# Where two groups of matmul operands begin in SBUF: projection weights and the ring of transposed inputs, in a graph-attention layer

## The reference, cut to what matters

```python
def layer(h, adjacency, W_left, b_left, W_self, b_self, W_right, b_right, gamma, beta):
    u = einsum('bld,bmd->blm', h, h) / sqrt(d)
    p = softmax(u, axis=-1)
    delta = p * adjacency
    attn = delta / (sum(delta, axis=2, keepdims=True) + 1e-10)
    h_left  = einsum('bld,ed->ble', h, W_left)  + b_left
    h_self  = einsum('bld,ed->ble', h, W_self)  + b_self
    h_right = einsum('bld,ed->ble', h, W_right) + b_right
    # above the diagonal: left; on it: self; below it: right
    ctx = attn_left @ h_left + diag(attn)[..., None] * h_self + attn_right @ h_right
    o = (ctx - mean(ctx)) / sqrt(var(ctx) + 1e-12) * gamma + beta
    return relu(o)
x = layernorm(x + layer(x, adj, ...))
```

## Time and profile before

| | us |
|---|---|
| median of 3 runs | 462.38 |
| lowest, highest | 462.02, 462.85 |
| the profiled execution | 462.62 |
| its span | 460.9 |
| TensorE busy in the span | 450.7 (98%) |
| VectorE, ScalarE, GpSimd busy | 383.0, 321.5, 209.4 |
| mean granted clock of TensorE | 0.995 |

### The profile page before, as it was taken

How to read it: one execution, slowest core, us unless ns; L and a number is a source line. 1 busy time by engine, 2 the same in 40 slices (tenths; PEclk the granted TensorE clock), 3 DMA queues, 4 the chain that set the end, 5 groups by cost and what they waited for, 6 DMA issues and landing times.

```text
span 460.9 us, 9449 instructions
## 1 busy us (share of the span) xinstructions
PE 450.7 (98%) x2639; PEld 448.4 (97%) x2639; DVE 383.0 (83%) x1117; ACT 321.5 (70%) x710; POOL 209.4 (45%) x293
## 2 busy tenths in 40 slices
PE   8999999999999999999999999999999999999992
PEld 8999999999999999999999999999999999999992
DVE  5877888888888878988878988878889887987876
ACT  6756677677677677678677677677677777767752
POOL 0144445543345553345554345554344653344542
PEclk9999999999999999999999999999999999999998
DMA  8765356566455665555666555566445566454322
GB/s 255 225 206 181 118 178 195 189 196 192 144 180 184 189 193 173 174 171 182 188 193 198 152 172 183 183 206 193 154 159 194 176 216 193 144 175 141 102 70 79
DMA packets 84134, 80.59 MB, mean 175 GB/s; under 512 B 7058, under 2 KB 76436, under 8 KB 84116
## 3 DMA queue, kind: packets, MB, share of 16 engines
q1 hardware_dynamic: 84112, 80.38, 54.7%
q10 hardware_dynamic: 4, 0.00, 0.0%
HBM read 52.04 MB, written 28.31 MB: 174 GB/s over the span
## 4 chain that ended last, share of the span: by engine, by line
issue 28%; POOL 21%; DVE 14%; PE 14%; ACT 11%; DMA 6%; SPq 5%; POOLq 0%; DVEq 0%; ACTq 0%
PE ps_proj L484 8%; POOL scaled L1112 7%; POOL shifted L1116 6%; DMA dt_raw<-dt_dram 5%; POOL rstd L1106 5%; ACT normed L639 4%; SPq L321 3%; DVE y_sb L867 3%; ACT ps_scores L590 3%; DVE proj_lo L819 3%; PE ps_ctx L528 3%; POOL dt_right L1100 2%; DVE delta L799 2%; DVE cross_turned L767 2%; POOL dt_left L1100 2%
## 5 line engine op out<-in xcount | busy, mean ns | idle before, releaser
L484 PE MATMUL ps_proj<-w_hi,xt_split 128*128 128x384 f32 x1152 | 304.8, 336 | 0.1
L484 PEld LDWEIGHTS ps_proj<-w_hi,xt_split 128*128 128x128 f32 x1152 | 209.1, 188 | 0.7 <-ACT ps_proj L609 0.5
L484 PE MATMUL ps_proj<-w_lo,xt_split 128*128 128x384 f32 x576 | 193.6, 336 | 0.0
L1106 POOL TENSOR_TENSOR rstd<-var_eps,minus_half 128x4 f32<-128x4 f32 x31 | 36.5, 1177 | 187.8 <-DVE var_eps L853 187.8
L484 PEld LDWEIGHTS ps_proj<-w_lo,xt_split 128*128 128x128 f32 x576 | 108.3, 188 | 0.0
L609 ACT ACTIVATE ps_proj<-bias 128x386 f32<-128x386 f32 (+1 forms) x188 | 90.5, 495 | 1.5 <-DVE proj_lo L819 1.2
L1112 POOL TENSOR_TENSOR scaled<-normed,gamma_sb 128x384 f32<-128x384 f32 x60 | 61.0, 1017 | 30.2 <-ACT normed L639 30.2
L613 ACT ACTIVATE proj_hi<-ps_proj 128x384 fp32r<-128x384 f32 x128 | 63.5, 497 | 11.3 <-PE ps_proj L484 11.0
L633 ACT ACTIVATE ps_ctx<-ps_proj,diag 128x386 f32<-128x386 f32 x64 | 35.7, 557 | 49.1 <-PE ps_proj L484 49.1
L819 DVE TENSOR_TENSOR proj_lo<-ps_proj,proj_hi 128x384 fp32r<-128x384 f32 x128 | 67.4, 544 | 2.1 <-ACT proj_hi L613 2.1
L1116 POOL TENSOR_TENSOR shifted<-scaled,beta_sb 128x384 f32<-128x384 f32 x61 | 61.9, 1015 | 2.5
(11 more groups left out here) (104 smaller groups left out, 640.2 us busy)
## 6 DMA issues: line engine op xcount, KB each, us to landing
x_sb<-in_x SPq DMA_DIRECT2D x32, 384.0 KB, 4.3
xt_sb<-in_x_t SPq DMA_DIRECT2D x31, 384.0 KB, 3.9
out_dram<-out_sb SPq DMA_DIRECT2D x31, 384.0 KB, 2.8
adj_sb<-in_adj SPq DMA_DIRECT2D x32, 256.0 KB, 4.4
dt_dram<-turned SPq DMA_DIRECT2D x31, 256.0 KB, 2.0
dt_raw<-dt_dram SPq DMA_DIRECT2D x124, 64.0 KB, 2.0
cross_dram<-cross_turned SPq DMA_DIRECT2D x29, 256.0 KB, 2.0
cross_raw<-cross_dram SPq DMA_DIRECT2D x116, 64.0 KB, 2.0
```

Of the source, the lines that this page charges most:

```text
L484: mm = nc.tensor.matmul(ps_proj[bank(at, g)][:, 0:H], stationary, moving[w][:, c, :], start=(clear and i == 0), stop=True, skip_group_chec ...
L1106: nc.gpsimd.tensor_tensor(rstd[at.slot(2)][:], var_eps[:], minus_half[:], ALU.pow).then_inc(rstd_ready, 1)
```

## The change

Three tiles are allocated that nothing reads or writes: 64 bytes ahead of the weights, 32 bytes ahead of `xt_split`, 32 bytes ahead of `dt_full`.

```diff
@@ -120,6 +120,8 @@
         ident = sb("ident", [P, P])
         zeros = sb("zeros", [P, HE], F32R)
         minus_half = sb("minus_half", [P, 2 * T])
+
+        sb("weights_place", [P, 16])
         w_raw = [sb(f"w_raw{w}", [P, C, H]) for w in range(3)]
         w_hi = [sb(f"w_hi{w}", [P, C, H], F32R) for w in range(3)]
         w_lo = [sb(f"w_lo{w}", [P, C, H], F32R) for w in range(3)]
@@ -131,6 +133,7 @@
         x_sb = [sb(f"x_sb{i}", [P, T, H]) for i in range(UNROLL)]
         xt_sb = [sb(f"xt_sb{i}", [P, C, L]) for i in range(UNROLL)]
         adj_sb = [sb(f"adj_sb{i}", [P, T, L]) for i in range(UNROLL)]
+        sb("xt_place", [P, 8])
 
         xt_split = [sb(f"xt_split{i}", [P, C, 2 * L], F32R) for i in range(UNROLL)]
         z_sum = [sb(f"z_sum{i}", [P, T]) for i in range(2)]
@@ -151,6 +154,7 @@
         cross_turned = sb("cross_turned", [P, Q * T * T * R])
         cross_raw = sb("cross_raw", [P, Q, T, T * R])
 
+        sb("dt_place", [P, 8])
         dt_full = sb("dt_full", [P, 2, T * T, P], F32R)
         dt_left = sb("dt_left", [P, 2, T, P], F32R)
         dt_right = sb("dt_right", [P, 2, T, P], F32R)
```

## The result

| | before | after |
|---|---|---|
| median, us | 462.38 | 467.29 |
| lowest to highest | 461.94 to 463.03 (5 runs) | 467.12 to 467.5 (5 runs) |
| span of the profiled execution | 460.9 | 465.4 |
| mean granted clock | 0.995 | 0.994 |

The ratio is 1.0099, with a 95% interval from 1.008 to 1.0119: the change makes the kernel slower by 1%, and the time lies in the predicted range of 456.5 to 468.5.

What follows compares the result with a forecast made beforehand. The prediction took TensorE's unbroken matmul stream to bound the kernel. Its terms for projections, scores, attention, other engines and DMA, each 0, summed to no change from the 462.38 us median: 462.4 us, range 456.5 to 468.5.

Steps and rivals of the forecast that it cites:

- What bounds the kernel: Whole kernel: TensorE, busy 98% of the span with 2.3 us of waits, sets the time by its matmuls' start-to-start distance.
- rival C: Projections: both operands beginning at 0 modulo 128 may meet, 173.3 to 176.7 ns each, +5.8 us, 468.2 us; chance 0.23.
- the prediction's own sign: Projections: the prediction is wrong if their distance changes by more than 0.53 ns.
- transfers and other engines: DMA, VectorE and ScalarE at new addresses: cost 0, hidden behind TensorE's unbroken stream.
- The likeliest case: Whole kernel: no change, within 0.2%, 461.5 to 463.3 us; chance 0.45.
- the term of the projections: 1728 projection matmuls with both operands moved to 0 modulo 128: taken as 0, bounds -23.0 and +5.8 us.
- The attention: Attention matmuls, whose operands keep their remainders: taken as 0, bounds 0.9 us either way.
- The scores: Scores matmuls in pieces, both operands moved from 32 to 0: taken as 0, bounds -3.5 and +0.9 us.
- The argument against C: Left and right projections of batch 0: 176.7 and 173.3 ns at the same remainders, so address alone does not set it.
- Rival A: Projections: aligned rows touch 12 blocks of 128 bytes instead of 13, saving 23.0 us, 439.4 us; chance 0.17.
- Rival B: TensorE's stream: other addresses give a shorter rhythm, 3.3 ns less, -5.8 us, 456.6 us (small form 461.2); chance 0.15.
- The formula of the Trainium skill: Projections: a page's gap for a warm stream, 162.5 ns against 173.3 measured; -18.7 us if unaligned operands explain it all.

Runs made afterwards that it cites:

- e5: Against the kernel before, only `xt_split` moved, to the same start modulo 512 as the weights (distance 0): 462.78 us, ratio 1.0006.
- f2: Against the kernel before, `xt_split` moved to begin 256 bytes above the weights modulo 512: 463.18 us, ratio 1.0017.
- f1: The change without the tile ahead of `xt_split`; weights at a multiple of 128, distance 96 as in the kernel before: 467.56 us, ratio 1.0109.
- e1: Against the kernel before, weights alone moved to 0 modulo 128, `xt_split` left at 32: 463.27 us, ratio 1.0013.
- e2: Against the kernel before, `xt_split` alone moved to 0 modulo 128, weights left at 64: 462.25 us, ratio 0.9991.
- e4: Against the kernel before, `xt_split` moved from 32 to 64 modulo 128, where the weights begin (distance 128 modulo 256): 467.25 us, ratio 1.0095.
- f3: Against the kernel before, `xt_split` moved to begin 384 bytes above the weights modulo 512: 466.83 us, ratio 1.0092.
- e8: Against the kernel before, `w_lo` and `xt_split` moved so only the low weight halves have distance 128, the high ones 192: 462.76 us, ratio 1.0006.
- e3: Against the kernel before, weights and `xt_split` both moved up by 32 bytes, their distance kept at 96: 463.34 us, ratio 1.0015.

## Why the prediction was right or wrong

**What bounds the kernel** was right. TensorE's stream sets the time, waits are no larger after, the clock is the same, and the whole difference is in the distance between matmuls. The time of 467.29 us lies in the range only because rival C was taken in; the forecast itself, 462.4 us, is missed by 4.9 us, and by the prediction's own sign (more than 0.53 ns a projection) it is wrong, with 2.8 ns measured. That transfers and other engines cost 0 at their new addresses was right too: `x_sb` lands after 4.4 us (before 4.3), `xt_sb` after 3.8 (before 3.9).

```profile
x_sb<-in_x SPq DMA_DIRECT2D x32, 384.0 KB, 4.4
xt_sb<-in_x_t SPq DMA_DIRECT2D x31, 384.0 KB, 3.8
```

**The likeliest case was wrong**, and the step that failed is the term of the projections: "I take 0, because the rows nearest to an aligned operand show no gain." Those rows, the `zeros` matmul and the scores in pieces, could only speak against a gain. They said nothing against a loss. A single matmul among others cannot show a rhythm, and the scores have both operands in one tile. Both operands of the `zeros` row begin at the same address, which is distance 0, and not the 128 modulo 256 that the change makes: remainders modulo 128 hid the difference. The measured term is 32 x 0.131 = 4.2 us. The 2.8 ns of a long stretch, taken for all 1728, would make 4.8 us, which is more than the whole span grew: the sixth group and the first matmuls behind the attention lose less. The attention, also put at 0, grew by about 0.5 us, within its bound of 0.9. The scores stayed at 0.

**Rival C had the place and nearly the size**: projections, +5.8 us for 3.33 ns each, measured +4.2 us of the +4.9 in all. Its mechanism did not hold, so the near size is luck. It said that both operands begin at 0 and meet; e5 and f2 begin alike modulo 256 and have the short rhythm. It also took the rhythm from batch 0, where each three take 0.53 us. That rhythm belongs to the distance 96, where f1 has it. The change has another, of 880 ns for five.

**The argument against C misread.** "Batch 0 has both rhythms at the same remainders, so the address alone does not set it" is true for a distance of 96, and f1 shows it once more. But I took it as evidence that addresses matter little. It was evidence that this stream has more than one rhythm and can change over, and neighbouring distances (112, 128) no longer have the short one in their long stretches. That the two rhythms at 96 come from standing beside that region is a reading, not shown. A smaller slip in the same place: the `zeros` row shows 0.18 us, which is 6 ns above the usual surplus and not 3 (the starts in ns give 177, which is 3).

**Rival A is refuted.** With weights at a multiple of 128 and a distance of 32 (e1), a row of 1536 bytes still takes 173.3 ns. That 13 blocks of 32 columns give exactly this was a coincidence, or has another cause. **Rival B** found no case: no distance tried went under 6.24 us for 36, so 173.3 ns looks like the floor of this stream. The formula of the Trainium skill, TensorE: Matmul & The Clock Gate, Back-to-back issue gap, N / 2.4 + 2.5 ns, is given there as the gap of an isolated matmul, not of a stream of weight loads and matmuls as here. The 162.5 ns that it would make of 384 columns, an estimate, was reached by none of these placements; none went under 173.3.

**What is shown, and what stays open.** Shown: the projections' spacing is the loss but for some 0.5 us, and only addresses changed. Neither operand's own start brings the loss alone (e1, e2, e4). The distance modulo 256 sorts all kernels but f1, and 128 is slow at three pairs of starts modulo 512, which are two modulo 256 (the change; e4 and f3). Distances 0, 32 and 192 were seen at one pair modulo 256 each. At 96 two kernels are fast and one is slow. Not shown is what it is in the chip. That the read of the moving columns and the load of the next weights disturb each other is an inference from the fact that a distance between those two operands counts. Nor is it known why the region lies around 112 and 128, how far it reaches above 128, and what picks the rhythm at 96.

## What to carry to other kernels

In a dense stream of fp32r matmuls, compare the starts in SBUF of the moving and the stationary operand with each other, modulo 256, and not each with a round number: here distances of 0, 32 and 192 bytes kept the short rhythm in long stretches, and 128 cost 1% of the kernel. An unrelated tile of a few bytes can shift that distance, so a difference of about 1% after such an edit, with no new wait and the same clock, is to be looked for in the start-to-start distance of the matmuls. If the same code runs at two spacings, as here in batch 0, the stream has more than one rhythm, and a few bytes can lose what it has: f1 has the distance of the kernel before and is slow.

## What the runs showed of the hardware that was not expected

- The delays of the stream repeat with a period of their own, which has nothing to do with the program's three: five matmuls (880 ns) at a distance of 128, two (353 ns, in the starts in ns) in f1.
- The start modulo 128 is not enough: e4 and e5 have the same starts modulo 128 and take 467.25 and 462.78 us.
- A third of the matmuls at the bad distance, spread through the stream (e8), cost nothing measurable: 462.76 us, 6.24 us for the 36.
- The same distance gave 6.24 us (before, e3) and 6.36 us (f1) for the same 36 matmuls, at the same granted clock.
